# One block for the feed-forward stage and the last stage, and the first batch's attention inside the last tile

## The reference

```python
x = x + tanh(g_xattn[0]) * xattn0(layernorm(x), ctx)   # 16 query heads, 4 key/value heads of 96
x = x + tanh(g_ffn[0])   * (layernorm(x) @ W4.T)       # W4: 1024x1024, dequantized, bf16
x = x + tanh(g_xattn[1]) * xattn1(layernorm(x), ctx)   # one head: softmax((y Wq'+bq)(ctx Wk'+bk)' / 32) @ ctx
x = x + tanh(g_ffn[1])   * (y @ W.T + b + lora(y))     # y = layernorm(x); rank 8/16/32/64 by top-1 gate
```

## Time and profile before

| | |
|---|---|
| time, median of 3 | 2038.38 us |
| time of the profiled execution | 2039.67 us |
| its span | 2037.9 us |
| busy PE, DVE, ACT, POOL | 96%, 51%, 36%, 36% |
| mean granted TensorE clock | 0.992 |

### The profile page before, as it was taken

How to read it: one execution, slowest core, us unless ns; L and a number is a source line. 1 busy time by engine, 2 the same in 40 slices (tenths; PEclk the granted TensorE clock), 3 DMA queues, 4 the chain that set the end, 5 groups by cost and what they waited for, 6 DMA issues and landing times. The chain is left out here.

```text
span 2037.9 us, 37346 instructions
## 1 busy us (share of the span) xinstructions
PE 1966.1 (96%) x13954; PEld 1298.7 (64%) x13968; DVE 1037.3 (51%) x1999; ACT 743.1 (36%) x1559; POOL 735.4 (36%) x722
## 2 busy tenths in 40 slices
PE   7999999998999999999999989999999959999998
PEld 3478888884666666666666545666766745666665
DVE  5555545533555555555555654343343436565564
ACT  4411111222555555555555651111111143444442
POOL 0000000111556565655565550011010147667662
PEclk9999999999999999999999999999999979999999
DMA  6533333333222222243222453231322456666661
GB/s 208 144 105 110 99 111 98 119 95 79 65 65 69 64 67 64 68 92 90 64 67 64 116 132 111 63 94 57 82 80 60 145 174 198 196 213 204 191 213 61
DMA packets 313217, 223.86 MB, mean 110 GB/s; under 512 B 247984, under 2 KB 284848, under 8 KB 308896
## 3 DMA queue, kind: packets, MB, share of 16 engines
q1 hardware_dynamic: 281840, 208.87, 35.5%
q10 hardware_dynamic: 31280, 13.64, 2.6%
HBM read 170.76 MB, written 51.65 MB: 109 GB/s over the span
## 5 line engine op out<-in xcount | busy, mean ns | idle before, releaser
L873 POOL TENSOR_TENSOR b_probT<-b_exp,b_probT 128x448 f16<-128x448 f32 (+2 forms) x256 | 265.1, 1038 | 301.8 <-ACT b_probT L935 301.8
L448 POOL TENSOR_TENSOR cT<-ctx_raw,cT 128x375 f16<-128x375 f32 x256 | 224.7, 898 | 132.5 <-ACT cT L443 132.5
L674 PE MATMUL a_pr<-a_yT,proj_q_p 128*128 128x256 f16 x2016 | 223.2, 273 | 0.0
L674 PEld LDWEIGHTS a_pr<-a_yT,proj_q_p 128*128 128x128 f16 x2016 | 197.3, 98 | 23.4
L1068 PE MATMUL b_kv_ps<-wkv_p,cT 128*128 128x384 f16 (+1 forms) x1152 | 210.6, 325 | 0.0
L1003 DVE TENSOR_REDUCE b_nmax<-b_mx_ps 112x2 f16<-112x974 f32 x128 | 149.6, 1169 | 109.5 <-PE b_mx_ps L1080 109.4
L1064 PE MATMUL b_kv_ps<-cT,wkv_p 128*128 128x375 f16 x1152 | 201.2, 326 | 3.7 <-PEq L465 3.7
L1105 PE MATMUL b_s_ps<-b_qT,b_kT 96*128 96x448 f16 (+5 forms) x768 | 189.6, 354 | 3.2 <-DMA b_qT<-b_nrow 2.2
L1120 PE MATMUL b_o_ps<-b_probT,b_v 128*128 128x448 f16 (+5 forms) x768 | 187.3, 351 | 4.4 <-POOL b_probT L873 4.4
L933 ACT ACTIVATE b_exp<-b_s_ps 128x448 f32<-128x448 f32 (+2 forms) x256 | 138.0, 539 | 127.6 <-PE b_s_ps L1105 121.1
L1812 PE MATMUL d_f_ps<-wo_early,d_y3T 128*112 128x512 f16 x768 | 173.8, 379 | 0.0
(11 more groups left out here) (202 smaller groups left out, 2816.2 us busy)
## 6 DMA issues: line engine op xcount, KB each, us to landing
ctx_raw<-in_ctx_t SPq DMA_DIRECT2D x32, 1500.0 KB, 7.9
d_cn_raw<-in_ctx_nat SPq DMA_DIRECT2D x30, 512.0 KB
b_qT<-qk_scratch SPq DMA_DIRECT2D x32, 336.0 KB, 4.5
o_scratch<-b_o SPq DMA_DIRECT2D x128, 84.0 KB, 1.9
qk_scratch<-a_heads SPq DMA_DIRECT2D x70, 144.0 KB, 2.1
x_scratch<-c_x SPq DMA_DIRECT2D x14, 512.5 KB, 3.6
raw<-in_x SPq DMA_DIRECT2D x14, 512.0 KB, 3.8
wkv_p<-in_x SPq DMA_DIRECT2D x14, 512.0 KB, 3.2
```

Of the source, the lines that this page charges most:

```text
L448: pool.tensor_tensor(cT[:, p, 1, k, 0:S], ctx_raw[:, k, :], cT[:, p, 0, k, 0:S], ALU.subtract).then_inc(split_lo, 1)
L674: last = mm(pr[:, n % PR, 0:GT * P], w[:, b, k, at * P:(at + 1) * P], yT[:, g % 2, a, k, :], start=(x == 0 and k == 0), stop=(x == 2 and k ...
L873: pool.tensor_tensor(pT[0:m, c, 1, :], ex[0:m, i % 2, :], pT[0:m, c, 0, :], ALU.subtract).then_inc(p_lo, 1)
```

## The change

One block: stage c's programs become functions `c_sync`, `c_gpsimd`, `c_scalar`, `c_vector`, `c_tensor`, which d's programs call first. No meeting of all engines is left between c and d. Batch 0's attention goes from d's slot 0 into c's slot 14. d's helpers (`softmax_head`, `exponent`, `scores_begun`, `probs_turned`, `attend1`, `attention_added`, ...) hold what stood in d's slots; `later(s)` leaves out slot 0:

```diff
+            def later(s):
+                return inside(s, B) and not (isinstance(s, int) and s == 0)
```

PE, slot 14 of c:

```diff
+                        if isinstance(s, int) and s == TILES:
+                            scores_begun(pe, 0, 0, 0)
+                            scores_ended(pe, 0)
                         if inside(s - 1, TILES):
                             pe.wait_ge(y2_ready, s)
                             turned(y2, y2tr)
...
                                 for m in range(h * KD // 2, (h + 1) * KD // 2):
+                                    if isinstance(s, int) and s == TILES and m == KD // 2:
+                                        probs_turned(pe, 0)
+                                    if isinstance(s, int) and s == TILES and m == KD // 2 + 1:
+                                        attend1(pe, 0)
```

ACT (slots 13 and 14), before it goes on to tile 13's t in slot 15 and then to d's slot 0 (`natural_high(1)`, unchanged) and slot 1 (y3T):

```diff
                         if isinstance(s, int) and s == TILES - 1:
+                            for k in range(KD):
+                                split_high(act, 0, B, k)
                             act.wait_ge(wo_done, 2 * TILES)
                             for c in range(3):
                                 staged_high(act, "n", c)
+                            act.wait_ge(wag_loaded, 16)
...
+                        if isinstance(s, int) and s == TILES:
+                            exponent(act, 0)
+                            for k in range(KD):
+                                split_high(act, 1, B + 1, k)
+                            for k in range(3, 5):
+                                staged_high(act, "w", k)
+                            probs_read(act, 0)
+                            staged_high(act, "w", 5)
+                            act.wait_ge(wb_loaded, 32)
...
+                            for k in range(6, KD):
+                                staged_high(act, "w", k)
```

DVE: in slot 13, `first_natural_low` (three, from POOL) and the low part of `wag`; in slot 14 pieces 0 to 2 of W first, then x2 and y2, `softmax_head`, the dot product and y2T's low part, `softmax_tail`, pieces 3 and 4 of W, and then:

```diff
                             for h in range(2):
+                                if isinstance(s, int) and s == TILES and h == 1:
+                                    attention_added(dve, 0, 0)
                                 cols = slice(h * HALF, (h + 1) * HALF)
                                 dve.wait_ge(t_done, 2 * (s - 1) + h + 1)
...
+                        if isinstance(s, int) and s == TILES:
+                            weight_low(dve, 5)
+                            dve.wait_ge(wb_hi, 1)
...
+                            for k in range(6, KD):
+                                weight_low(dve, k)
```

SP. The order of the staged pieces is changed, batch 0's loads start in slot 13 as soon as tile 12's output projection is done, and SP takes over from the ACT queue the stores of t of tiles 12 and 13:

```diff
-            STAGED = [("w", k) for k in range(6)] + [("n", c) for c in range(3)] + [("b", 0), ("w", 6), ("w", 7)]
+            STAGED = [("n", c) for c in range(3)] + [("w", k) for k in range(6)] + [("b", 0), ("w", 6), ("w", 7)]
...
+                def store_turned(eng, t):
+                    eng.wait_ge(tT_hi, t + 1)
+                    eng.wait_ge(tT_lo, t + 1)
+                    for part in range(2):
+                        eng.dma_start(t_s[part, :, :, rows(t, P)], tT[:, part, :].rearrange("p (k r) -> p k r", k=KD)
+                                      ).then_inc(t_stored, 16)
...
+                        if isinstance(s, int) and s == TILES:
+                            load_raw(sp, B + 1, 1)
+                            for k in range(3, 6):
+                                load_staged(sp, "w", k)
                         if inside(s - 1, TILES):
+                            store_rows(1 - p, s - 1)
+                        if isinstance(s, int) and s == TILES - 1:
+                            for k in range(3):
+                                load_staged(sp, "w", k)
+                        if isinstance(s, int) and s == TILES:
+                            sp.wait_ge(t_stored, 64)
+                            for part in range(2):
+                                sp.dma_start(rowsT[1][:, part, :, :], t_s[part, :, :, Q:2 * Q]).then_inc(tx_loaded[1], 16)
+                            sp.wait_ge(x2_stored[0], 16 * (TILES // 2))
+                            load_biases(sp)
+                            store_turned(sp, s - 2)
                             load_staged(sp, "b", 0)
+                            for k in range(6, KD):
+                                load_staged(sp, "w", k)
+                        if isinstance(s, int) and s == SLOTS - 1:
+                            load_second(sp)
+                            store_turned(sp, s - 2)
```

More of the change, by code:

```diff
@@ L1368, in slot @@
                             act.activation(tT[:, 0, :], t32[:, :], ACT.Copy).then_inc(tT_hi, 1)
[L1369 to L1374 removed]
+                        if inside(s - 2, TILES) and not (isinstance(s, int) and s >= TILES):
+                            store_turned(act, s - 2)
                         if inside(s - 1, TILES):
@@ new lines, in probs_read, with scores @@
+            def probs_read(act, s):
+                act.wait_ge(ptr, s + 1)
+                for c, (a, n) in enumerate(CH):
+                    for part in range(2):
+                        o = (part * 3 + c) * Q
+                        act.activation(pT1[0:n, part, c, :], tr1[0:n, 0, o:o + Q], ACT.Copy).then_inc(pT_ready, 1)
+            def scores(pe, p, n):
+                for k in range(KD):
+                    last = mm(s1_ps[0:Q, 0:S], rowsT[p][:, PASSES[n][0], k, :], cT[:, p, PASSES[n][1], k, 0:S],
+                              start=(n == 0 and k == 0), stop=(n == 2 and k == KD - 1))
+                return last
@@ new lines, in scores_begun, with scores_ended, probs_turned @@
+            def scores_begun(pe, j, p, s):
+                pe.wait_ge(split_lo, KD * (s + 1 + B))
+                pe.wait_ge(tx_loaded[p], rows_in(j, p))
+                wait(pe, exped1, s)
+                for n in range(2):
+                    scores(pe, p, n)
+            def scores_ended(pe, p):
+                scores(pe, p, 2).then_inc(scored1, 1)
+            def probs_turned(pe, s):
+                for part in range(2):
+                    pe.wait_ge((p1_hi, p1_lo)[part], s + 1)
+                    for c, (a, n) in enumerate(CH):
+                        o = (part * 3 + c) * Q
+                        last = pe.transpose(tr1[0:n, 0, o:o + Q], pp[:, part, a:a + n], ident[0:Q, 0:Q])
+                last.then_inc(ptr, 1)
@@ new lines, in attend1 @@
+            def attend1(pe, s):
+                pe.wait_ge(cn_lo, 3 * (s + 1))
+                pe.wait_ge(pT_ready, 6 * (s + 1))
+                for h in range(2):
+                    wait(pe, x3_ready, 2 * (s - 1) + h + 1)
+                    for i, (a, b) in enumerate(PASSES):
+                        for c, (_, n) in enumerate(CH):
+                            last = mm(a_ps[0:Q, h, :], pT1[0:n, a, c, :],
+                                      cn[0:n, b, c, h * HALF:(h + 1) * HALF],
+                                      start=(i == 0 and c == 0), stop=(i == 2 and c == 2))
+                    last.then_inc(attended, 1)
@@ L1658, in slot @@
                                        ACT.Copy).then_inc(y3T_hi, 1)
-                    if inside(s, B):
-                        act.wait_ge(biased, s + 1)
-                        wait(act, normed, s)
-                        act.activation(ex[:, 0:S], s_ps[0:Q, 0:S], ACT.Exp, bias=sm[:, 2:3], scale=SCALE,
-                                       accum_out=sm[:, 3:4]).then_inc(exped, 1)
-                    if isinstance(s, int) and s == 0:
-                        for k in range(6, KD):
-                            staged_high(act, "w", k)
+                    if later(s):
+                        exponent(act, s)
                     if inside(s - 1, B):
```

373 lines of the change are left out of this document (180 added, 193 removed).

## The result

| | before | after |
|---|---|---|
| median of 20 runs each | 2040.66 us (2035.17 to 2046.87) | 2036.67 us (2033.93 to 2041.15) |
| ratio, with its 95% interval | 1 | 0.9983 (0.9975 to 0.9990) |
| profiled execution, its span | 2039.67, 2037.9 us | 2038.35, 2036.5 us |
| mean granted clock | 0.992 | 0.989 |

The kernel became faster by 3.5 us (2.0 to 5.1, from the ratio). The forecast was 10.9. The changed kernel's own median lies 0.67 us above the end of the predicted range, and the gain is less than 0.3%, the bound that the prediction set for a change that can be told; with 20 runs of each the interval excludes 1. The forecast counted from 2038.38, the median of 3 runs; 20 runs of the same kernel give 2040.66. So the time was 9.2 us above the forecast of 2027.5, and the gain 7.4 us short of it.

The account below looks back on a forecast made before the run. PE's work plus its gaps was taken as the bound, and a chain of waits to set the gate product's start. That start moves from 1691.87 to 1681.0, minus 10.9 us from 2038.38: 2027.5, bounds 2023 to 2034, range 2020 to 2036.

Parts of the forecast that it names:

- the chain hides: Rival: SP's natural load or ACT's y3T gets past what stands ahead; gate product at 1665, time about 2011; chance 0.06.
- Slots get longer: Rival: in stage d's slots loads land later and PE loses 1.3 us in each of 13; 2045 and more; chance 0.07.
- T - M: From tile 13's first feed-forward matmuls to slot 1's gate product `d_ag_ps`, whose start was to move from 1691.87 to 1681.0.
- E: End of tile 13's folded projection on PE, predicted at 1659.0, by 1.5 us either way.
- step 7: Landing of the third piece of batch 1's natural context: 6.0 us from its issue, to 1676.9.
- slot 1: Stage d from the gate product to the start of batch 2's scores (S): unchanged at 19.96 us, bounds -1.5 and +2.
- steps 1 to 6: From the projection's end through bias, W pieces 5 and 7, t's split and store to batch 1's natural load: 1659.7 to 1670.0.
- step 8: ACT reads batch 1's three natural pieces (2.95 us), then y3T's high part (0.90): 1679.9 and 1680.8.
- turn of y2 at 1640.8, PE idle 1.8 us: Before tile 13's folded projection: y2 0.6 us later, as low parts of three W pieces stand ahead of x2 on DVE.
- 11.0 us at full clock: Tile 13's folded projection on PE: 16 and 176 matmuls, 1.06 + 10.00 us, instead of 12.38.
- tile 13 waits as well: Rival: batch 1's turned context lands late and delays tile 13's turns; 4 to 10 us late, 2031 to 2038; chance 0.15.
- the biases: Among the edits that the prediction costed at nothing.

Follow-up runs that it names:

- e3: Changed kernel with POOL making the low part of tile 12's t before the root for y2, not behind it: ratio 0.9965, 2034.17 us.
- e4: Changed kernel with SP issuing batch 2's loads only after batch 1's natural pieces have landed: ratio 0.9982, 2036.73 us.
- e1: Changed kernel with batch 1's natural load issued on SP before the store of tile 13's t, not behind it: ratio 0.9937, 2027.57 us.
- e6: Changed kernel with e1, e2 and e3 together: ratio 0.9933, 2025.15 us.
- e8: Changed kernel with batch 0's scores, softmax and attention all behind tile 13's folded projection: ratio 1.0029, 2046.02 us.
- e5: e1 with every natural piece of 119 rows in stage d loaded as 112 and 7 rows: ratio 0.9941, 2026.74 us.
- e11: The kernel of e1 run again, on the same chip as e12: ratio 0.9947, 2029.32 us.
- e12: The kernel of e6 run again, on the same chip as e11: ratio 0.9922, 2024.52 us.
- e9: e6 with batch 1's natural pieces behind both exps on ACT and behind the probabilities' low part on POOL: ratio 0.9914, 2023.80 us.
- e2: Changed kernel with the low part of W piece 5 made before attention_added on DVE: ratio 0.9971, 2034.11 us.

## Why the prediction was wrong, by its steps

**The way was right.** One idle stretch of PE before the gate product, ended by y3T, ACT waiting ahead of it for `d_cn_raw`, SP's store just before that load, softmax hidden, later slots as before: each was predicted and is in the rows above. The chain rival to the contrary ("the chain hides") is out: ACT waits 14.68 us. "Slots get longer" is out too, 21.68 us for a later slot. T - M fell by 2.7 us where 10.9 was forecast. The step that failed is the sizing of the chain's terms: the 8.2 us between, and 1.3 behind T, come mainly from three of them, E, step 7 and slot 1:

| term | predicted | measured | off | shown by |
|---|---|---|---|---|
| end of the folded projection, E - M | 27.6 | 31.6 | +4.0 | e3: 28.8 |
| steps 1 to 6, E to the first natural issue | 11.0 | 11.4 | +0.4 | the chain |
| step 7, first issue to ACT's start | 6.9 | 10.95 | +4.05 | the chain; e4, e1: 9.0, 10.4 |
| step 8, ACT's start to T | 4.1 | 3.8 | -0.3 | the chain |
| slot 1, T to S | 19.96 | 21.28 | +1.3 | the same in e1 to e6 |

**E, +4.0: "turn of y2 at 1640.8, PE idle 1.8 us".** PE was idle for 4.11. The scaling of y2 fell beside POOL's split of tile 12's t (2.53 instead of 0.81, in e3 0.81 again), and that is most of the turn's delay (11.56 us from M, predicted 9.41; 10.10 in e3). The rest is in "11.0 us at full clock": 192 in 11.06 us are 5.5 for the first 96, with the 0.6 us of waiting 6.1; they took 8.10, in e3 6.88. Windows of 2 us of the kernel after, in the columns of the earlier trace rows:

```profile
1640.00:1642.00 2.00, 0.17 (x2) 0.17 (x2) 2.00 (x2) 0.00 (x0) 1.23 (x1) 1.00 1.03 420
1642.00:1644.00 2.00, 1.00 (x8) 0.69 (x7) 1.89 (x6) 0.96 (x2) 0.00 (x0) 0.68 0.41 168
1644.00:1646.00 2.00, 1.88 (x18) 1.89 (x19) 1.93 (x5) 2.00 (x7) 0.00 (x0) 0.50 0.50 178
```

The granted clock was 1.00 (2.4 GHz) in the idle stretch and fell to 0.50 (1.2 GHz) when PE went on. I had the clock stay up as the scores filled the first gap. Of the 4.0 us at E, e3 gives back 2.8. Of the 1.2 left, 0.8 is the half clock that e3 still has (6.88 us where I had 6.1). This is the case "tile 13 waits as well" in its size (4 us late at E), but not in its mechanism: that case named batch 1's turned context, and the turns and attention had no gap.

**Step 7, +4.05.** I took the wait of one piece issued by itself, 6.0 us, and added it to the third issue. The rows of the kernel before held the right comparison: batch 1's same three pieces, issued one straight after the other, went from 1679.04 to ACT's start at 1687.95, 8.9 us, and I used it only for the upper bound, from the third piece on. Measured: 9.0 with nothing behind (e4) to 12.05 (e8), in the kernel after 10.95. Of the 4.05 us, 0.9 is the later third issue and 3.1 the time from it. Holding back the loads behind gave 1.9; why the rest takes 9 us stays open. The prediction's reading by the row count (7 engines for 119 rows) is neither borne out nor ruled out by e5.

**Slot 1, +1.3.** I had "the biases" at nothing. Before, DVE scaled them ahead of y3T's low part, beside the turn of y3, as these rows of the kernel before show:

```profile
1689.63 0.75 DVE L1788 TENSOR_SCALAR d_tg_b<-d_tg_b,tg 128x1024 f32<-128x1024 f32 x1
1690.41 3.04 DVE L1790 TENSOR_TENSOR d_x3b<-d_x,d_tg_b 112x1024 f32<-112x1024 f32 x1
1693.37 1.08 DVE L1761 TENSOR_TENSOR d_y3T<-d_tr,d_y3T 128x896 f16<-128x896 f32 x1
```

After, they stand behind y3T's low part, ahead of batch 1's softmax (`d_tg_b` is the last line of the chain above, and then):

```profile
1690.23 3.03 DVE L1675 TENSOR_TENSOR d_x3b<-d_x,d_tg_b 112x1024 f32<-112x1024 f32 x1
```

The slot takes 21.28 or 21.29 us from T in after and in e1 to e6, e8, e11 and e12, with waits before T from 9.1 to 22.7 us. So the length doesn't come from the idle time. That it is the 4.1 us of bias work in front of the softmax is argued from the order of the rows; no run moved it alone. Half clock is a rival that is nearly as long in the kernel after: PE took 5.42 us for the first 16 feed-forward matmuls where 3.64 was usual, and then waited only 0.29 for the probabilities. Against it: in e1 they took 4.35, PE waited 1.36, and the slot was as long. In e9, where POOL was idle beside it, the second instruction took 1.23 us instead of 3.03.

From S on both profiles run alike, but for the tail: 43.4 us from the start of the last scores against 42.2, as its first 24 feed-forward matmuls took 6.90 us against 5.37. This differs from profile to profile (7.04 in e3, 5.37 in e1), so it is chance. M itself came 1.1 us earlier. With -2.7 + 1.3 - 1.1 + 1.2 the two profiled executions should differ by -1.3, and they do (2039.67 and 2038.35). The medians differ by 3.5 (2.0 to 5.1). What the 2 us between them are is open.

Whether e2's 4.8 us in the profile and 2.5 in time, e3's 1.7 and 3.7, and e4's 1.7 and none are more than noise can't be said: each is one profile, and the intervals of two ratios leave some 3 us either way.

## What to carry to other kernels

When a meeting of all engines is taken out, read every queue across the old border and write down what stands ahead of the first load of the next stage: here a store on SP, ready 10 us after the last matmul, stood in front of a load that could have gone at once, and moving one line brought more than the whole change (9.4 against 3.5 us). Price a group of transfers by a group in the trace, from its first issue to its first reader, and not by one of its members. And an instruction that is moved on POOL is to be laid beside DVE's instructions at its new place, not only beside its own queue's.

## What the runs showed of the hardware

A small DVE instruction can be held for a whole run of POOL instructions. The 4-column `d_gp` in e9 over all slots (count, then least, mean and longest ns):

```profile
L1877 DVE TENSOR_SCALAR d_gp<-d_gp,d_small x16: 229/898/7142, 1674.1 to 2008.0; 112x4 f32<-112x4 f32 x16
```

Its shortest took 229 ns; in the kernel before its longest was 901 ns, the length of the one POOL instruction beside it. In e9 it began 0.02 us after POOL's 0.90 us, three splits of 6.28 us stood behind that on POOL, and it ended 0.03 us after the last of the four. The Trainium skill (SBUF — State Buffer, section "SBUF: two separate sides") describes the port pair that the two engines share as a lock that one instruction holds alone; the trace agrees, and adds that between POOL's instructions DVE did not get it.

PE's clock fell to 0.51 (1.2 GHz) in e3 behind idle stretches of 2.65 and 1.12 us with 8 transposes (1.09 us) between them, as it did behind 4.11 and 1.12 in the kernel after:

```profile
1640.00:1642.00 2.00, 1.40 (x14) 1.40 (x15) 1.93 (x6) 2.00 (x6) 0.00 (x0) 0.51 0.63 258
```
